# Expert results scattered one expert later, in sets of five transfers that wait once for the first products, with places and gates copied by VectorE

## The chip, the cores and the metric

One core of one Trainium2 chip runs the whole program. The metric is the device time of one execution in microseconds; the number given for a kernel is the median of its runs. A profile is one execution more, with a trace of every instruction.

## The reference, cut to what matters

The program is one pre-norm transformer block on x of shape (4, 1024, 128), 4096 tokens: a windowed attention, then a mixture of experts. Only the second part is touched by the change.

```python
x = x + attention(layernorm(x))
xf = layernorm(x).reshape(4096, 128)
shared = silu(xf @ sg) * (xf @ su) @ sd
# router: 4 of 32 experts per token, gates = softmax of their scores,
# each expert takes at most capacity = 640 (token, choice) pairs
h = silu(einsum('ecd,edh->ech', buf, wg)) * einsum('ecd,edh->ech', buf, wu)   # 256 hidden
out_e = einsum('ech,ehd->ecd', h, wd)
routed[token] += gate * out_e[expert, place]
x = x + shared + routed
```

## The kernel before, in words

**What the stages are.** Up to about 400 us the attention runs (16 pairs of 128-token tiles, software pipelined), together with the router. GpSimd sends every token row, with its pair number and its gate behind it (130 numbers), to its slot in `expert_slots` in DRAM by indirect DMAs (L479). Then come the 32 experts, and last the combination: the four results of each token are loaded from `pair_results` (L425), added to x (L1450, L1456, L1140, L1142) and stored (L798).

**One expert.** An expert has 640 slots, five tiles of 128 rows (`ST` = 5), and hidden width 256, two halves h. `lagged_steps` calls `expert_step(en, e, ed)` on TensorE, VectorE and ScalarE with three experts at once: `en` is one ahead (its slots are turned round and split in two parts), `e` is the present one (products with the gate and the up weights), and `ed` is one behind (product with the down weights, and the results read out). A call is named a stage below. The stages 3 and later run in a hardware loop of two stages per turn; buffers come in pairs, chosen by the expert's parity b.

- TensorE in one stage: five transposes of `xg` (L1101), `gate_up(0)` on the first 320 slots (L1090, 12 matmuls: two halves, gate and up, three partial products each), the down product of `ed` (L1116, 10 products recorded as 20 matmuls), `gate_up(1)` on the other 320 slots (12 more). Each quarter of a `gate_up` adds one to `gu_done`; the last matmul of the down product adds one to `down_done`. The down product waits for `h_mul` (all products of `ed`) and for `y_evac` (the banks of the expert before have been read out).
- ScalarE in one stage: the cast of the weights of `en` (L768), `silu(0)` (two times L761), then the results of `ed` out of the banks, times their gates, into `yout` (five times L780), then `silu(1)` (two times L761). L780 waits for `down_done` and for `y_sent[b]`, which says that the results that stood in this `yout` buffer have landed in DRAM.
- VectorE in one stage: the places of `ed` as whole numbers, `yidx` (L1470), four operations that split `xgT` (L1479, L1482), the products `times_up(0)` (two times L1464, one `h_mul` each), the split of the weights (L1489), `times_up(1)`, and the copy of places and gates from `xg` into `ypair` (L1497), which lets SyncE load the next slots into `xg`.
- GpSimd does nothing but the scatter: for each expert five indirect DMAs (L605) that write the rows of `yout` to `pair_results` at the places in `yidx`. Each one waits for its own tile of results (`y_evac`), so that the first one leaves behind the first L780. The fourth also waits for `h_mul` to reach 4e + 8, which is the last product of expert e + 1.
- SyncE loads the slots (L331), the gate and up weights (L324, L325) and the down weights (L328). L328 waits for `down_done`, so its start shows when SyncE saw that semaphore.

In numbers of experts: while stage e runs, L780 reads out expert e - 1, and GpSimd scatters expert e - 1 in the same stage.

The lines that set the order around the change:

```python
def silu(ch): ... act.wait_ge(S.gu_done, ...); a.activation(hact[...], bank[2 + h], Silu)   # L758 to L762
silu(0)
if ed is not None: ...   # wait down_done, y_sent, ypair_ready, then five times L780
silu(1)
```

Of the kernel before, what the change touches and what calls it, by code (L numbers as in the profile page):

```python
# [14 lines left out]
P = 128  # L15
# [20 lines left out]
NE, NGR, TOPG, TOPK = 32, 8, 4, 4  # L36
# [49 lines left out]
def block_kernel(nc, x, w_qkv, w_out, group_c, expert_c, bias, w_g, w_u, w_d, s_g, s_u, s_d, const, out, where, cap):  # L86
# [53 lines left out]
    with ExitStack() as ctx:  # L140
        def sb(name, shape, dt=F32, stack=None):
            return (stack or ctx).enter_context(nc.sbuf_tensor(name, shape, dt))
# [98 lines left out]
        xg = sb("xg", [P, 2, ST, ROW])  # L241
        ypair = sb("ypair", [P, 2, ST, 2])
        yidx = sb("yidx", [P, 2, ST], U32)

# [20 lines left out]
        pos_read slots slot_ready sh_gu sh_act sh_mul sh_down sh_added  # L265
        xgT_done xgT_hi xgT_lo wgu_hi wgu_lo gu_done h_act h_mul down_done y_evac ypair_ready yidx_ready half_sum comb_step sum_done sum_out stored""".split()
        S = namedtuple("Semaphores", names)(*[sem(n) for n in names])
# [14 lines left out]
        def hold(eng):  # L282

            eng.nop(nofuse=True)
# [156 lines left out]
        def _(pool):  # L441
# [152 lines left out]
            pool.wait_ge(S.zeroed, 16 * NZERO)  # L594
            def scatter(e, c, more):
                pool.wait_ge(S.yidx_ready, e + 1)
                for j in range(ST):
                    if j == 3 and more:


                        pool.wait_ge(S.h_mul, 4 * e + 8)

                    pool.wait_ge(S.y_evac, ST * e + (j + 1))
                    hold(pool)
                    g.indirect_dma_start(  # L605
                        out=pairs_d, out_offset=bass.IndirectOffsetOnAxis(ap=yidx[:, c, j:j + 1], axis=0),
                        in_=yout[:, c, j, :], in_offset=None, bounds_check=N * TOPK - 1,
                        oob_is_err=False).then_inc(y_sent[c], 16)

            with pool.Fori(0, NE // 2 - 1) as i:  # L610
                for c in range(2):
                    scatter(2 * i + c, c, True)
            scatter(NE - 2, 0, True)
            scatter(NE - 1, 1, False)


        @block.scalar
        def _(act):
# [138 lines left out]
            def expert_step(en, e, ed):  # L757
# [11 lines left out]
                if e is not None:  # L769

                    wait(act, S.down_done, e.n - 1)
                    silu(0)
                if ed is not None:
                    act.wait_ge(S.down_done, ed.n + 1)

                    wait(act, y_sent[ed.b], 16 * ST * ed.half)
                    act.wait_ge(S.ypair_ready, ed.n + 1)
                    hold(act)
                    for j in range(ST):
                        a.activation(yout[:, ed.b, j], bank[6 + j // 4][:, j % 4 * D:(j % 4 + 1) * D], ACT.Copy,  # L780
                                     scale=ypair[:, ed.b, j, 1:2]).then_inc(S.y_evac, 1)
                if e is not None:
                    silu(1)

# [362 lines left out]
        def _(dve):  # L1147
# [310 lines left out]
            def expert_step(en, e, ed):  # L1458
# [7 lines left out]
                if ed is not None:  # L1466

                    dve.wait_ge(S.ypair_ready, ed.n + 1)
                    wait(dve, y_sent[ed.b], 16 * ST * ed.half)
                    v.tensor_copy(yidx[:, ed.b], ypair[:, ed.b, :, 0]).then_inc(S.yidx_ready, 1)  # L1470
                if en is not None:
# [19 lines left out]
                if e is not None:  # L1491
                    times_up(1)
                if en is not None:

                    wait(dve, S.yidx_ready, en.n - 1)
                    wait(dve, S.y_evac, ST * (en.n - 1))
                    v.tensor_copy(ypair[:, en.b], xg[:, en.b, :, D:ROW]).then_inc(S.ypair_ready, 1)  # L1497
# [37 lines left out]
```

## Time and profile before

| | us |
|---|---|
| median of 3 runs | 732.65 (728.56 to 733.83) |
| the profiled execution's own time | 729.37 |
| its span in the trace | 726.9 |
| TensorE busy | 574.7 (79%) |
| VectorE busy | 421.1 (58%) |
| ScalarE busy | 323.7 (45%) |
| GpSimd busy | 344.3 (47%) |
| mean granted clock | 0.893 |

A row of the timeline gives the start, the length, the engine, the line and the tiles of one instruction, or of several of the same kind in a row (x2 and so on, with the length from the first start to the last end), and in brackets how long the engine had been idle before it and who ended that. Starts are measured; the ends of matmuls are modelled. SPq is SyncE's own queue. "Remote" or "an unknown queue" is a releaser that the profile could not name. L605 is POOL's part of one transfer; the data moves later.

### The profile page before, as it was taken

The numbers are of one execution on the slowest core, as the hardware profiler recorded it, in microseconds if no ns is written. First come the engines' busy times: TensorE is split into PE (matmuls) and PEld (weight loads), VectorE is DVE, ScalarE is ACT, GpSimd is POOL, SyncE is SP. The second block draws the span as 40 slices with busy tenths as digits, with TensorE's granted clock in tenths as the row PEclk, the third lists the DMA queues.
The fourth block names the chain that finished last, engine by engine and source line by source line (L and its number), as shares of the span: only waits on it lengthen the run. The fifth ranks groups of instructions, "written<-read, shape, count | busy, mean of one in ns | idle before, by whom it ended". The sixth has DMA issues, their size and how long they took to land.

```text
span 726.9 us, 20783 instructions
## 1 busy us (share of the span) xinstructions
PE 574.7 (79%) x7427; PEld 463.1 (64%) x7427; DVE 421.1 (58%) x1284; ACT 323.7 (45%) x830; POOL 344.3 (47%) x393
## 2 busy tenths in 40 slices
PE   2559887888888898777658898788888888888775
PEld 1336665666666666555435787678887888787653
DVE  4757696776787778654445744444444444444155
ACT  4326764665655656445433333444333333333310
POOL 6210034555554445556577055555555555555610
PEclk9669998998888889998989999999999889999897
DMA  9987877865555554300000333332334433332069
GB/s 284 227 233 189 212 209 217 256 184 168 137 157 171 173 159 122 96 20 18 11 9 9 96 115 98 99 87 82 111 99 121 132 118 110 117 88 76 16 249 334
DMA packets 78649, 98.33 MB, mean 135 GB/s; under 512 B 11329, under 2 KB 59231, under 8 KB 78448
## 3 DMA queue, kind: packets, MB, share of 16 engines
q1 hardware_dynamic: 64512, 82.91, 39.7%
q0 software_dynamic: 9216, 12.02, 5.3%
q10 hardware_dynamic: 4848, 2.40, 1.1%
q8 instruction: 49, 0.80, 0.5%
q14 instruction: 24, 0.20, 0.1%
HBM read 50.00 MB, written 54.30 MB: 143 GB/s over the span
## 4 chain that ended last, share of the span: by engine, by line
PE 47%; another core or an unknown queue 13%; issue 12%; ACT 11%; DMA 5%; SPq 5%; DVE 4%; POOL 2%; ACTq 1%; POOLq 0%; DVEq 0%
PE banks L1090 8%; PE banks L1116 6%; PE banks L907 6%; ACT yout L780 4%; DMA rload<-pair_results 3%; PE banks L857 3%; PE banks L978 3%; ACT hact L761 3%; PE banks L849 2%; PE banks L875 2%; SPq L352 2%; PE banks L925 2%; PE banks L888 2%; PE banks L881 2%
## 5 line engine op out<-in xcount | busy, mean ns | idle before, releaser
L605 POOL DMA_INDIRECT pair_results<-yout,yidx x160 | 156.0, 975 | 138.0 <-ACT yout L780 95.2
L479 POOL DMA_INDIRECT expert_slots<-xfe,sidx x128 | 126.0, 984 | 135.1 <-DVE mx L1204 52.3
L1090 PE MATMUL banks<-xgT_parts,wgu_parts 128*128 128x320 f32 x768 | 148.0, 345 | 35.6 <-ACT hact L761 32.9
L1090 PEld LDWEIGHTS banks<-xgT_parts,wgu_parts 128*128 128x128 f32 x768 | 126.1, 208 | 46.9 <-ACT hact L761 36.8
L1464 DVE TENSOR_TENSOR hact<-hact,banks 128x320 f32<-128x320 f32 x128 | 57.0, 481 | 137.2 <-ACT hact L761 126.2
L780 ACT ACTIVATE yout<-banks,ypair 128x128 f32<-128x128 f32 x160 | 44.7, 371 | 135.1 <-remote 79.3
L1204 DVE TENSOR_REDUCE mx<-banks 128x8 f32<-128x1024 f32 x64 | 78.1, 1221 | 37.3 <-PE banks L857 36.4
L648 ACT ACTIVATE pt<-banks 128x512 f32<-128x512 f32 x128 | 69.7, 598 | 51.3 <-PE banks L888 33.4
L1116 PE MATMUL banks<-wdn,hact 128*128 128x128 f32 x640 | 82.3, 287 | 1.9 <-DVE hact L1464 1.9
L1116 PEld LDWEIGHTS banks<-wdn,hact 128*128 128x128 f32 x640 | 82.0, 206 | 2.2 <-issue 2.2
L907 PE MATMUL banks<-pt,vals 128*32 128x64 f32 x2048 | 58.2, 235 | 22.0 <-issue 19.4
L761 ACT ACTIVATE hact<-banks 128x320 f32<-128x320 f32 x128 | 53.3, 452 | 37.6 <-PE banks L1090 26.6
L907 PEld LDWEIGHTS banks<-pt,vals 128*32 128x32 f32 x2048 | 41.2, 117 | 35.1 <-issue 28.0
L525 POOL TENSOR_TENSOR pout<-pin,powers 128x6 f32<-128x6 f32 x16 | 22.3, 1395 | 50.5 <-DVE pin L1285 50.4
L857 PE MATMUL banks<-kS,qS 64*64 64x128 bf16 x1024 | 35.0, 231 | 13.3 <-issue 13.3
L857 PEld LDWEIGHTS banks<-kS,qS 64*64 64x64 bf16 x1024 | 26.9, 114 | 24.8 <-issue 19.7
L653 ACT COPY pvT<-banks 128x512 f32<-128x512 f32 x32 | 18.7, 585 | 53.5 <-PE banks L907 47.3
L849 PE MATMUL banks<-maskq_b,ident_b 64*64 64x512 bf16 x256 | 27.6, 422 | 13.7 <-DVE mx L1204 8.8
L1479 DVE CAST xgT_parts<-banks 128x512 fp32r<-128x512 f32 x64 | 28.3, 483 | 4.7 <-issue 3.3
L1101 PE MATMUL banks<-cst,xg 128*128 128x128 f32 x160 | 25.6, 274 | 6.0 <-issue 3.5
L978 PE MATMUL banks<-cst,pvT 128*128 128x128 f32 x128 | 25.6, 366 | 4.6 <-ACT pvT L653 4.5
L888 PE MATMUL banks<-qS,kS 64*128 64x64 bf16 x1024 | 28.7, 200 | 0.1
(155 smaller groups left out, 957.7 us busy)
## 6 DMA issues: line engine op xcount, KB each, us to landing
expert_slots<-xg SPq DMA_DIRECT2D x8, 1300.0 KB, 9.5
xg<-expert_slots SPq DMA_DIRECT2D x32, 325.0 KB
pair_results<-zero SPq DMA_DIRECT2D x8, 1024.0 KB
rload<-pair_results SPq DMA_DIRECT2D x16, 512.0 KB, 9.5
kS<-rotated_keys SPq DMA_DIRECT2D x32, 240.0 KB
qS<-rotated_queries SPq DMA_DIRECT2D x32, 192.0 KB
wgu<-in_L_ffn_wg_dram SPq DMA_DIRECT2D x32, 128.0 KB
wgu<-in_L_ffn_wu_dram SPq DMA_DIRECT2D x32, 128.0 KB
```

The lines of the kernel that those rows point to most:

```text
L479: g.indirect_dma_start(out=slots_d, out_offset=bass.IndirectOffsetOnAxis(ap=sidx[:, m % NB, j, k:k + 1], axis=0), in_=xfe[:, m % NB, j, k, ...
L605: g.indirect_dma_start(out=pairs_d, out_offset=bass.IndirectOffsetOnAxis(ap=yidx[:, c, j:j + 1], axis=0), in_=yout[:, c, j, :], in_offset= ...
L648: a.activation(pt[:, u], bank[2 + st][:, :], ACT.Exp, scale=QK_SCALE).then_inc(S.exp_done, 1)
L761: a.activation(hact[:, e.b, h, ch * CH:(ch + 1) * CH], bank[2 + h][:, 0:CH], ACT.Silu)\
L780: a.activation(yout[:, ed.b, j], bank[6 + j // 4][:, j % 4 * D:(j % 4 + 1) * D], ACT.Copy, scale=ypair[:, ed.b, j, 1:2]).then_inc(S.y_evac, 1)
L857: last = mm(bank[st][hb * WIN:(hb + 1) * WIN, i * P:(i + 1) * P], qS[rows, p % NX, 4 * c + i, at:at + WIN], kS[rows, p % NX, 4 * c + i, at ...
L907: last = mm(bank[6][32 * (h % 4):32 * (h % 4 + 1), to:to + WIN], vals[:, m % 2, j, hb, h, :], pt[:, 4 * j + NS * c + st, at:at + WIN], sta ...
L978: last = nc.tensor.transpose(bank[6 + j][:, q * P:(q + 1) * P], pvT[:, j, q * P:(q + 1) * P], ident)
L1090: last = mm(bank[2 + 2 * w + h][:, 0:CH], wgu_parts[:, e.b, wp, w, h * P:(h + 1) * P], xgT_parts[:, e.b, xp, ch * CH:(ch + 1) * CH], start ...
L1116: last = mm(bank[6 + j // 4][:, j % 4 * D:(j % 4 + 1) * D], hact[:, ed.b, h, j * P:(j + 1) * P], wdn[:, ed.b, h, :], start=(h == 0), stop= ...
L1204: v.tensor_reduce(mx[:, j, :, 4 * c:4 * c + 4], bank_pairs[0][:, :, :].rearrange("p s (c j) -> p s c j", c=4), AX.X, ALU.max).then_inc(S.p ...
L1464: v.tensor_tensor(hs, hs, bank[4 + h][:, 0:CH], ALU.mult).then_inc(S.h_mul, 1)
```

## The change

It does five things, all in the expert stages.

- ScalarE does `silu(0)` and `silu(1)` first and reads out the results of `ed` after them.
- A second small buffer `ysend` takes the pair (place, gate) from `ypair`. VectorE fills it at the start of a stage (L1469 of the changed kernel), after the read-out of the expert before is over. L780 takes its gates from there (it is L782 now).
- The whole-number places `yidx` are made at the end of a stage, after `times_up(1)` (L1495), with the wait for `y_sent`.
- The copy into `ypair` waits for `ysend` of the expert that stood there, no longer for `y_evac` and `yidx`.
- GpSimd waits once per expert, then issues five transfers without a wait between them. It waits for `h_mul` to reach 4p - 2 with p = e + 3, which is the second product of expert e + 2 (its `times_up(0)`), for `yidx` and for all five tiles of `y_evac`. So expert e is scattered in stage e + 2. For the last two experts p is 32, so that the experts 29, 30 and 31 all wait for the second product of expert 31.

```diff
-            def scatter(e, c, more):
+            def scatter(e, c, half, more, products):
+                pool.wait_ge(S.h_mul, 4 * products - 2)
                 pool.wait_ge(S.yidx_ready, e + 1)
+                pool.wait_ge(S.y_evac, ST * (e + 1))
+                hold(pool)
                 for j in range(ST):
-                    if j == 3 and more:
-                        pool.wait_ge(S.h_mul, 4 * e + 8)
-                    pool.wait_ge(S.y_evac, ST * e + (j + 1))
-                    hold(pool)
                     g.indirect_dma_start(
...
                 if e is not None:
                     wait(act, S.down_done, e.n - 1)
                     silu(0)
+                    silu(1)
                 if ed is not None:
                     act.wait_ge(S.down_done, ed.n + 1)
                     wait(act, y_sent[ed.b], 16 * ST * ed.half)
-                    act.wait_ge(S.ypair_ready, ed.n + 1)
+                    act.wait_ge(S.ysend_ready, ed.n + 1)
...
-                                     scale=ypair[:, ed.b, j, 1:2]).then_inc(S.y_evac, 1)
-                if e is not None:
-                    silu(1)
+                                     scale=ysend[:, ed.b, j, 1:2]).then_inc(S.y_evac, 1)
...
                 if ed is not None:
                     dve.wait_ge(S.ypair_ready, ed.n + 1)
-                    wait(dve, y_sent[ed.b], 16 * ST * ed.half)
-                    v.tensor_copy(yidx[:, ed.b], ypair[:, ed.b, :, 0]).then_inc(S.yidx_ready, 1)
+                    wait(dve, S.y_evac, ST * (ed.n - 1))
+                    v.tensor_copy(ysend[:, ed.b], ypair[:, ed.b]).then_inc(S.ysend_ready, 1)
...
                 if e is not None:
                     times_up(1)
+                if ed is not None:
+                    wait(dve, y_sent[ed.b], 16 * ST * ed.half)
+                    dve.wait_ge(S.ysend_ready, ed.n + 1)
+                    v.tensor_copy(yidx[:, ed.b], ysend[:, ed.b, :, 0]).then_inc(S.yidx_ready, 1)
                 if en is not None:
-                    wait(dve, S.yidx_ready, en.n - 1)
-                    wait(dve, S.y_evac, ST * (en.n - 1))
+                    wait(dve, S.ysend_ready, en.n - 1)
                     v.tensor_copy(ypair[:, en.b], xg[:, en.b, :, D:ROW]).then_inc(S.ypair_ready, 1)
```

GpSimd in the loop over the experts, one expert before (what stands in brackets are the semaphores that the row waits for):

```order
L603 ISA [waits yidx_ready]
L605 DMA pair_results<-yout,yidx 16384x128 [waits y_evac]
L603 REGISTER_ALU
L605 DMA pair_results<-yout,yidx 16384x128 [waits y_evac]
L603 REGISTER_ALU
L605 DMA pair_results<-yout,yidx 16384x128 [waits y_evac]
L601 ISA
L603 REGISTER_ALU [waits h_mul]
L605 DMA pair_results<-yout,yidx 16384x128 [waits y_evac]
L603 REGISTER_ALU
L605 DMA pair_results<-yout,yidx 16384x128 [waits y_evac]
```

Each transfer has its own wait, and the fourth waits for products. The same engine and place in the changed kernel:

```order
L599 REGISTER_ALU [waits h_mul]
L600 REGISTER_ALU [waits yidx_ready]
L603 DMA pair_results<-yout,yidx 16384x128 [waits y_evac]
L603 DMA pair_results<-yout,yidx 16384x128 x4
```

All waits stand ahead of the first transfer now, and the one for products comes first.

ScalarE at the head of the loop, as a piece of the difference (minus is before, plus the changed kernel; L761 is the silu, L780 and L782 the read-out of the results):

```order
-L761 ACTIVATE hact<-banks 128x320 x2
-L780 ACTIVATE yout<-banks,ypair 128x128 x5
-L761 ACTIVATE hact<-banks 128x320 x2
+L761 ACTIVATE hact<-banks 128x320 x4
+L782 ACTIVATE yout<-banks,ysend 128x128 x5
 L768 CAST wgu_parts<-wgu 128x512
```

The read-out moved behind the second pair of silus. VectorE between two stages of the loop:

```order
-L1497 COPY ypair<-xg 128x10
-L1470 CAST yidx<-ypair 128x5
...
+L1495 CAST yidx<-ysend 128x5
+L1498 COPY ypair<-xg 128x10
+L1469 COPY ysend<-ypair 128x10
+L1478 CAST xgT_parts<-banks 128x512
```

One small copy was added, and the making of `yidx` went ahead of the copy into `ypair`.

## Rows read from the trace of the kernel before

**Rows 1.** The page: the chain that ended last, by engine.

```profile
PE 47%; another core or an unknown queue 13%; issue 12%; ACT 11%; DMA 5%; SPq 5%; DVE 4%; POOL 2%; ACTq 1%; POOLq 0%; DVEq 0%
```

**Rows 2.** Who waited for whom, 420 to 688: us in total, times, longest.

```profile
ACT yout L780 <- remote: 79.3, 17, 5.0
ACT yout L780 <- PE banks L1116: 48.7, 13, 4.3
```

**Rows 3.** Timeline of one stage of the loop, and the next read-out.

```profile
488.70 1.40 ACT L780 ACTIVATE yout<-banks,ypair 128x128 f32<-128x128 f32 x5 [4.26 <-PE banks L1116]
489.89 0.97 POOL L605 DMA_INDIRECT pair_results<-yout,yidx  x1 [2.63 <-ACT yout L780]
491.16 0.97 POOL L605 DMA_INDIRECT pair_results<-yout,yidx  x1 [0.30 <-issue]
491.35 0.16 DVE L1497 COPY ypair<-xg 128x10 f32<-128x10 f32 x1
492.51 2.39 PE L1116 MATMUL banks<-wdn,hact 128*128 128x128 f32 x20
493.08 0.87 DVE L1464 TENSOR_TENSOR hact<-hact,banks 128x320 f32<-128x320 f32 x2
494.66 2.00 PE L1090 MATMUL banks<-xgT_parts,wgu_parts 128*128 128x320 f32 x12
494.99 0.97 POOL L605 DMA_INDIRECT pair_results<-yout,yidx  x1 [0.30 <-issue]
497.32 0.38 SPq L328 DMA_DIRECT2D wdn<-in_L_ffn_wd_dram  x1
497.41 1.40 ACT L780 ACTIVATE yout<-banks,ypair 128x128 f32<-128x128 f32 x5 [4.70 <-remote]
```

**Rows 4.** Timeline of the first stages of the loop of experts, no transfer of GpSimd under way.

```profile
416.77 2.39 PE L1116 MATMUL banks<-wdn,hact 128*128 128x128 f32 x20
419.28 1.40 ACT L780 ACTIVATE yout<-banks,ypair 128x128 f32<-128x128 f32 x5 [2.31 <-PE banks L1116]
423.05 2.39 PE L1116 MATMUL banks<-wdn,hact 128*128 128x128 f32 x20
427.92 1.40 ACT L780 ACTIVATE yout<-banks,ypair 128x128 f32<-128x128 f32 x5 [4.13 <-remote]
```

**Rows 5.** Timeline in the attention, around one single transfer.

```profile
204.88 0.78 PE L907 MATMUL banks<-pt,vals 128*32 128x64 f32 x35 [0.42 <-issue]
205.50 0.97 POOL L479 DMA_INDIRECT expert_slots<-xfe,sidx  x1 [0.95 <-ACT xfe L714]
206.93 0.59 ACT L653 COPY pvT<-banks 128x512 f32<-128x512 f32 x1 [1.52 <-PE banks L907]
```

**Rows 6.** Timeline of the stage in which the transfers stopped after three.

```profile
610.79 1.40 ACT L780 ACTIVATE yout<-banks,ypair 128x128 f32<-128x128 f32 x5 [4.98 <-remote]
616.13 0.49 DVE L1464 TENSOR_TENSOR hact<-hact,banks 128x320 f32<-128x320 f32 x1 [0.49 <-PE banks L1090]
617.09 0.98 POOL L605 DMA_INDIRECT pair_results<-yout,yidx  x1 [1.59 <-issue]
618.51 1.40 ACT L780 ACTIVATE yout<-banks,ypair 128x128 f32<-128x128 f32 x5 [2.70 <-PE banks L1116]
622.24 0.97 POOL L605 DMA_INDIRECT pair_results<-yout,yidx  x1 [0.30 <-issue]
624.30 0.49 DVE L1464 TENSOR_TENSOR hact<-hact,banks 128x320 f32<-128x320 f32 x1 [2.41 <-PE banks L1090]
628.72 1.40 ACT L780 ACTIVATE yout<-banks,ypair 128x128 f32<-128x128 f32 x5 [3.14 <-PE banks L1116]
```

**Rows 7.** Windows: busy of PE, PEld, DVE, ACT, POOL, granted clock, DMA share, GB/s.

```profile
420.00:680.00 260.00, 221.17 (x1463) 206.88 (x1462) 121.79 (x325) 100.97 (x297) 146.27 (x150) 0.92 0.35 102
```

**Rows 8.** Timeline of the end of the experts.

```profile
677.62 0.49 DVE L1464 TENSOR_TENSOR hact<-hact,banks 128x320 f32<-128x320 f32 x1 [1.09 <-ACT hact L761]
693.73 0.97 POOL L605 DMA_INDIRECT pair_results<-yout,yidx  x1 [0.30 <-issue]
```

More of the change, by code:

```diff
@@ L242, in block_kernel @@
         ypair = sb("ypair", [P, 2, ST, 2])
+        ysend = sb("ysend", [P, 2, ST, 2])
         yidx = sb("yidx", [P, 2, ST], U32)
@@ L265, in block_kernel @@
         pos_read slots slot_ready sh_gu sh_act sh_mul sh_down sh_added
-        xgT_done xgT_hi xgT_lo wgu_hi wgu_lo gu_done h_act h_mul down_done y_evac ypair_ready yidx_ready half_sum comb_step sum_done sum_out stored""".split()
+        xgT_done xgT_hi xgT_lo wgu_hi wgu_lo gu_done h_act h_mul down_done y_evac ypair_ready ysend_ready yidx_ready half_sum comb_step sum_done sum_out stored""".split()
         S = namedtuple("Semaphores", names)(*[sem(n) for n in names])
@@ L608, in scatter @@
                         oob_is_err=False).then_inc(y_sent[c], 16)
-            with pool.Fori(0, NE // 2 - 1) as i:
+            for e in range(2):
+                scatter(e, e, 0, True, e + 3)
+            with pool.Fori(0, NE // 2 - 2) as i:
                 for c in range(2):
-                    scatter(2 * i + c, c, True)
-            scatter(NE - 2, 0, True)
-            scatter(NE - 1, 1, False)
+                    scatter(2 * i + (c + 2), c, i + 1, True, 2 * i + (c + 5))
+            scatter(NE - 2, 0, NE // 2 - 1, True, NE)
+            scatter(NE - 1, 1, NE // 2 - 1, False, NE)
         @block.scalar
```

## The prediction

> **What bounds the kernel now.** The chain that ended last, on the page, is 47% TensorE and 13% "another core or an unknown queue" [rows 1]. A program on one core has no other core, so the first question is who that is. The list of who waited for whom answers: over the expert stages ScalarE stood 79.3 us ahead of L780 for a "remote" releaser and 48.7 us for L1116 [rows 2]. Together that is 128 us in 30 read-outs, more than half of every stage.
>
> The timeline of one stage shows what it waited for. L780 begins at 488.70 and at 497.41 [rows 3], and over the 23 stages from 427.92 [rows 4] to 628.72 [rows 6] the mean distance is 200.80 / 23 = 8.73 us. Follow the piece at 497.41 back. It needs the down product, whose last matmul is modelled to end at 492.51 + 2.39 = 494.90. TensorE did not stop there: gate_up(1) starts at 494.66. Yet L780 starts only at 497.41, and SyncE, which waits for the same `down_done` and for nothing of `yout`, starts L328 at 497.32 [rows 3]. Two engines see `down_done` at the same moment, 2.4 us after the product. What ends just before? The last of GpSimd's five transfers began at 494.99, 2.33 us before L328. In the stages before any transfer, the same product ends at 416.77 + 2.39 = 419.16 and L780 follows at 419.28, after 0.12 us [rows 4]. So TensorE's `down_done` reaches the others only when a running set of transfers is over. One transfer alone does it too: in the attention L907 ends at 205.66, a transfer starts at 205.50, and the copy that waits for L907 starts at 206.93, 1.43 us after that transfer and 1.27 us after the product [rows 5].
>
> With this the stage closes on itself: read-out to first transfer 489.89 - 488.70 = 1.19, five transfers 494.99 - 489.89 = 5.10, last transfer to next read-out 497.41 - 494.99 = 2.42. The sum is 8.71, the stage. TensorE alone would be faster: with no transfer under way two down products stand 423.05 - 416.77 = 6.28 us apart [rows 4], at the full clock; at the mean granted clock of 0.92 [rows 7] that is 6.8. It idles for the rest.
>
> **The change part by part.** *Read-out behind silu(1).* No cost of its own, the same seven instructions. It takes 1.40 us [rows 3] out from between gate_up(1) and `times_up(1)`; behind the five L780 now stand the weights' cast and `silu(0)` of the next stage. The next down product needs `y_evac`; it comes 6.3 us after the present one at the earliest, and the read-out ends, by the rows' lengths, about 2.4 + 2.0 + 0.5 + 1.4 = 6.3 us after the present one began. Just covered; if not, some tenths.
>
> *Places and gates by VectorE.* One more copy of 0.16 us per expert (as L1497 [rows 3]), 32 x 0.16 = 5 us of an engine that was busy 121.79 of 260 us [rows 7]. It lies ahead of the casts of the next expert, whose result is needed a stage later. I count 0. The move of `yidx` behind `times_up(1)` costs 0: GpSimd needs it a half stage later. Queued behind its wait for `y_sent` are L1498 and through it SyncE's next slots; the set it asks for was sent more than a stage earlier, and 7.4 us after its start it has landed.
>
> At 491.35 a fp32 copy of VectorE (L1497) ran inside a transfer of GpSimd at 491.16, and both kept their lengths, 0.16 and 0.97 [rows 3]. The Trainium skill ("SBUF — State Buffer", the box on "DVE blocks DMA" in "SBUF: two separate sides") says that such a copy locks GpSimd out of the shared port, so that descriptors cannot be written. By that rule each added copy could delay a set by its 0.16 us, 29 x 0.16 = 4.6 us in the sum; the trace shows no such delay, and the sum goes by the trace.
>
> *Transfers one expert later.* This is the term that counts. Before, a set began 1.19 us after the read-out and ran beside the down product and gate_up(1). Now it begins after `times_up(0)`. In rows 3 that ends at 493.08 + 0.87 = 493.95, and from such a product to a waiting transfer it is 617.09 - (616.13 + 0.49) = 0.47 us [rows 6]. So a set starts 493.95 + 0.47 - 492.51 = 1.9 us after the down product began, and lasts 5.10 + 2.33 = 7.4 us until TensorE's messages are through. Within that lie the end of the down product, gate_up(1), the transposes and the next gate_up(0). The loop is now: last part of gate_up(0) seen, `times_up(0)`, five transfers, and again. Bounds for it:
> - Nothing that matters is held: TensorE at the mean clock, 6.8, hardly over GpSimd's own 5 x 1.27 = 6.4.
> - The last part of gate_up(0) is held to the end of the set, as `down_done` is now: 5.10 + 2.33 + 0.49 (the product) + 0.47 = 8.4. If the third part is held as well, a silu of the same 128x320 tile comes in, taken as long as the product: 8.9.
> - gate_up(1) is held as well. That is what the stage of rows 6 shows, the one in which the transfers halted for 1.59 us and then went on at 617.09, 1.2 us after the down product had begun: a product of `times_up(1)` came only at 624.30, 2.06 us after the last transfer at 622.24, and the stage took 628.72 - 618.51 = 10.2.
>
> Which? In rows 3 results that fell in the first part of a set were used at once: gate_up(0) was over when the down product began at 492.51, 2.6 us into the set, and its products ran at 493.08. What was held, the down product at 494.90, fell 5.0 us into it. Of the new stage gate_up(0) falls there, from about 4 us after the set's start on (the rest of the down product 0.5, gate_up(1) 2.0, the transposes, then quarter by quarter). That is the middle case, 8.4. But stages differ: the one up to 618.51 took 618.51 - 610.79 = 7.7 [rows 6], and where a set starts late against TensorE, gate_up(0) slips ahead of the held part. I take two stages of three at 8.4 and one at 7.7, mean 8.2.
>
> *Sum.* From 8.73 to 8.2 in 28 stages: -15. The first set leaves a stage later, so one stage more runs as those of rows 4: -2. At the end experts 29, 30 and 31 all wait for the second product of expert 31, at 677.62 + 0.49 = 678.11 [rows 8]. If the 15 transfers follow closely, the last starts at 678.11 + 0.47 + 14 x 1.27 = 696.4, against 693.73 [rows 8]: +2.7. If each set waits for a held down product, there is one set of 5.1 us and one gap of 2.33 + 1.19 more in it, so up to +7. I take +4, and nothing hides it: the final loads wait for the last transfer. Together -13. The profiled execution took 729.4, 3.3 below the median of 732.65; 729.4 - 13 = 716.4 stands for 719.7 on the scale of the medians. I say 720.
>
> **The rivals.**
> - *TensorE takes over (F).* Held messages fall where nobody waits, and a stage takes 6.8 to 7.4. For it: gate_up(0) was free for 4 us of each set. Against it: the set is longer than TensorE's whole work for a stage, so something always falls in its last part. 28 x (8.73 - 7.1) = 46 less, with the start and the end 44: 689. The Trainium skill ("TensorE: Matmul & The Clock Gate", "The cost: per-tile semaphore tail") gives for a matmul's semaphore a tail of some tens of ns, 25 + 4.7 + 26.3 = 56 for one; by that nothing would be held at all, and this rival would be the forecast. The 2.4 us of rows 3 contradict it here beside transfers; the 0.12 of rows 4 agrees without them.
> - *A wait takes the place of the one removed (N).* Two parts are held, the stage is 8.6 to 8.9, or the late read-out keeps the down product waiting. 28 stages give -3 to +5, start and end +2: 732 to 740, and 728 where the end costs nothing.
> - *gate_up(1) is held (S), slower.* One mechanism: the last quarter of gate_up(1) is not seen before the set is over; then `times_up(1)`, the next down product, VectorE's four operations for the next expert and `times_up(0)` all queue behind it before GpSimd may start. Rows 6 price it at 10.2 for a stage. Such a stage costs 1.5 more than before where the others gain 0.53, so with +2 for start and end it decides from a share s with 28 x (1.5 s - 0.53 (1 - s)) + 2 = 0, s = 0.23. At half of the stages it is 28 x 0.49 + 2 = +16, 748; at all of them 776. For it: only there did a set start so shortly after a down product at full clock, as it will now. Against: a late set shifts itself away from gate_up(1), since the set waits for products and TensorE does not.
> - *The change doesn't do what it says (P).* The 15 transfers at the end and the first stage can't eat more than 7 us, so it isn't a case of its own; it belongs to N.
>
> **How the numbers follow.** Forecast 0.40 (710 to 728: faster by over 1% in 0.32 of it, the rest within), F 0.12, N 0.20 (0.16 within 1%, 0.04 above), S 0.28. One per cent, 7.3 us, is about what a measurement of this kernel can tell from no change. Faster by over 1%: 0.32 + 0.12 = 0.44. Within 1%: 0.08 + 0.16 = 0.24. Slower: 0.04 + 0.28 = 0.32. The range leaves out F's lower half and the part of S with more than half of the stages: 702 to 750. The likeliest case's own range is 710 to 728.
>
> **What would show it.** Right: ScalarE's wait ahead of the read-out (128 us) is gone or small; the first transfers of two sets stand 8.2 to 8.4 apart; VectorE waits ahead of the second product of `times_up(0)` until about 2.3 us after a fifth transfer; the last transfer starts between 696 and 701 less the gain. F: the sets stand 6.8 to 7.4 apart and TensorE has no gaps. S: VectorE's wait ends 2.1 us after the fifth transfer ahead of `times_up(1)`, TensorE waits in gate_up(0) for L1464, and sets stand over 9 us apart. The forecast would be wrong at its root if TensorE's results were seen late with no transfer under way, or at once in the last part of a set.

## The result and the profile after

The changed kernel takes 759.4 us (median of 4 runs, 756.97 to 762.92) beside 733.24 for the kernel before (728.56 to 737.79). The ratio is 1.044, with a 95% interval of 1.0384 to 1.0495: slower, outside the range of the prediction. Ratios here and below are taken over undisturbed executions alone and so can differ a little from the ratio of the medians. The profiled execution has a span of 755.2 us, 28.3 more than before, at a mean clock of 0.876.

The list of who waited for whom (us in total, times, longest), 420 to 715:

```profile
ACT hact L761 <- remote: 111.6, 21, 11.8
POOL pair_results L603 <- DVE hact L1464: 111.4, 18, 24.2
DVE hact L1464 <- ACT hact L761: 88.9, 35, 10.2
```

The same list of the kernel before has for GpSimd, 420 to 688:

```profile
POOL pair_results L605 <- ACT yout L780: 94.9, 30, 19.8
POOL pair_results L605 <- DVE hact L1464: 2.8, 2, 2.5
```

The "remote" wait of [rows 2] has moved from the read-out to the silu, and single waits are longer, 11.8 us against 5.0. GpSimd waited for read-outs before, 94.9 us, and hardly for products (2.8 us). Now it stood 111.4 us for products. The window that answers to [rows 7]:

```profile
420.00:710.00 290.00, 219.71 (x1473) 205.82 (x1471) 128.14 (x357) 103.34 (x306) 146.24 (x150) 0.88 0.30 91
```

TensorE is as busy as before (219.71 against 221.17), in 30 us more. The granted clock is lower (0.88 against 0.92), but the time was lost in idling and not in longer work. The timeline of one of the bad stages, against [rows 3]:

```profile
463.01 1.39 ACT L782 ACTIVATE yout<-banks,ysend 128x128 f32<-128x128 f32 x5
463.49 0.97 POOL L603 DMA_INDIRECT pair_results<-yout,yidx  x1 [3.13 <-DVE hact L1464]
463.69 2.00 PE L1090 MATMUL banks<-xgT_parts,wgu_parts 128*128 128x320 f32 x12
465.53 2.39 PE L1116 MATMUL banks<-wdn,hact 128*128 128x128 f32 x20
467.79 0.49 DVE L1464 TENSOR_TENSOR hact<-hact,banks 128x320 f32<-128x320 f32 x1 [1.22 <-remote]
468.59 1.14 POOL L603 DMA_INDIRECT pair_results<-yout,yidx  x1 [0.30 <-issue]
470.03 0.97 POOL L603 DMA_INDIRECT pair_results<-yout,yidx  x1 [0.30 <-issue]
475.14 0.97 POOL L603 DMA_INDIRECT pair_results<-yout,yidx  x1 [0.30 <-issue]
477.81 0.77 ACT L761 ACTIVATE hact<-banks 128x320 f32<-128x320 f32 x2 [10.34 <-remote]
477.88 0.38 SPq L329 DMA_DIRECT2D wdn<-in_L_ffn_wd_dram  x1
478.30 3.57 PE L1090 MATMUL banks<-xgT_parts,wgu_parts 128*128 128x320 f32 x12 [6.00 <-ACT hact L761]
478.45 1.40 ACT L782 ACTIVATE yout<-banks,ysend 128x128 f32<-128x128 f32 x5
```

Read it from the product at 467.79. It ends at 468.28, and it is the second product of `times_up(0)`, the trigger of the next set. The running set's fifth transfer begins only at 468.59. So the next set follows without a gap (470.03), and there are ten transfers in a row, from 463.49 to 475.14. The down product ends at 465.53 + 2.39 = 467.92; SyncE (L329) sees it at 477.88, 9.96 us later and 2.74 us after the tenth transfer began. The silus of gate_up(1) wait 10.34 us for the same moment, and the read-outs stand 478.45 - 463.01 = 15.44 us apart. Behind its 6.00 us of idling TensorE needs 3.57 us for a gate_up that took 2.00; the granted clock from 478 to 482 is 0.50, the lower of its two levels.

Not everything is held to the end of the run. The gate_up(0) of 463.69 ends at 465.69, 2.2 us into the set, and its last product starts at 467.79: 2.1 us late, but ahead of the fifth transfer. That is what lets the next set join.

From the read-out at 427.34 to the last at 715.04 there are 30 distances. Eight are of this kind, 14.4 to 15.5 us, together 120.7. The other 22 take (287.7 - 120.7) / 22 = 7.59. Before, the 30 from 427.92 to 687.46 took 259.54, 8.65 each. So most stages gained 1.06 us, and eight lost 6.4: 8 x 6.44 - 22 x 1.06 = +28.2. (One of the 22, near the end, took 11.1; there too two sets join, at 695.42 and 701.80. The other 21 took 7.4.) Of the eight, five are ten transfers joined as above; in the other three the second set begins 7.1 to 7.2 us after the first, as here:

```profile
494.01 0.97 POOL L603 DMA_INDIRECT pair_results<-yout,yidx  x1 [4.56 <-DVE hact L1464]
496.42 2.39 PE L1116 MATMUL banks<-wdn,hact 128*128 128x128 f32 x20
499.11 0.97 POOL L603 DMA_INDIRECT pair_results<-yout,yidx  x1 [0.30 <-issue]
501.15 0.97 POOL L603 DMA_INDIRECT pair_results<-yout,yidx  x1 [1.07 <-issue]
505.43 0.39 SPq L329 DMA_DIRECT2D wdn<-in_L_ffn_wd_dram  x1
506.25 0.97 POOL L603 DMA_INDIRECT pair_results<-yout,yidx  x1 [0.30 <-issue]
508.65 0.62 ACT L782 ACTIVATE yout<-banks,ysend 128x128 f32<-128x128 f32 x2
```

The down product ends at 496.42 + 2.39 = 498.81. SyncE sees it at 505.43, 6.6 us later and ahead of the second set's fifth transfer (506.25). So here the message outlasts the first set but not the second. Why it comes out just there, no run shows.

The end, against [rows 8]:

```profile
711.11 0.97 POOL L603 DMA_INDIRECT pair_results<-yout,yidx  x1 [3.23 <-DVE yidx L1495]
722.59 0.97 POOL L603 DMA_INDIRECT pair_results<-yout,yidx  x1 [0.30 <-issue]
```

The last transfer starts at 722.59 instead of 693.73, 28.9 later. Behind it the program takes 32.6 us to its end (755.2 - 722.59), before 33.2.

### The profile page after: what moved, and what is told of

The parts are those of the page before. It is cut to its first block, busy times and chain, and to the rows that moved or that the text cites. A ratio compares the mean times of both kernels' runs of the same rounds, so it can differ in the third digit from the quotient of the medians.

```text
span 755.2 us, 20577 instructions
## 1 busy us (share of the span) xinstructions
PE 577.3 (76%) x7427; PEld 463.4 (61%) x7427; DVE 427.1 (57%) x1316; ACT 324.9 (43%) x830; POOL 345.8 (46%) x393
## 4 chain that ended last, share of the span: by engine, by line
PE 48%; another core or an unknown queue 13%; issue 12%; ACT 6%; DMA 5%; DVE 5%; SPq 5%; POOL 5%; POOLq 0%; ACTq 0%; DVEq 0%
PE banks L1090 13%; PE banks L907 6%; PE banks L1116 6%; DMA rload<-pair_results 3%; SPq L353 2%; POOL expert_slots L480 2%; PE banks L849 2%; PE banks L875 2%; PE banks L978 2%; PE banks L888 2%; PE banks L925 2%; PE banks L857 2%; PE banks L935 2%; PE banks L881 1%
## 5 line engine op out<-in xcount | busy, mean ns | idle before, releaser
L603 POOL DMA_INDIRECT pair_results<-yout,yidx x160 | 156.0, 975 | 166.7 <-DVE hact L1464 111.4
L1090 PEld LDWEIGHTS banks<-xgT_parts,wgu_parts 128*128 128x128 f32 x768 | 124.1, 205 | 66.4 <-ACT hact L761 45.6
L1464 DVE TENSOR_TENSOR hact<-hact,banks 128x320 f32<-128x320 f32 x128 | 59.7, 483 | 152.7 <-ACT hact L761 89.2
L761 ACT ACTIVATE hact<-banks 128x320 f32<-128x320 f32 x128 | 54.7, 447 | 196.2 <-remote 111.6
L907 PE MATMUL banks<-pt,vals 128*32 128x64 f32 x2048 | 62.9, 236 | 24.8 <-issue 22.9
L907 PEld LDWEIGHTS banks<-pt,vals 128*32 128x32 f32 x2048 | 43.3, 116 | 40.8 <-issue 34.7
L782 ACT ACTIVATE yout<-banks,ysend 128x128 f32<-128x128 f32 x160 | 44.7, 381 | 7.2 <-PE banks L1116 7.2
L857 PE MATMUL banks<-kS,qS 64*64 64x128 bf16 x1024 | 32.3, 230 | 9.1 <-issue 9.1
L875 PE MATMUL banks<-eye_b,maskq_b 64*128 64x512 bf16 x128 | 27.9, 433 | 1.0 <-ACT pt L648 1.0
```

The source lines that it names most:

```text
L603: g.indirect_dma_start(out=pairs_d, out_offset=bass.IndirectOffsetOnAxis(ap=yidx[:, c, j:j + 1], axis=0), in_=yout[:, c, j, :], in_offset= ...
L761: a.activation(hact[:, e.b, h, ch * CH:(ch + 1) * CH], bank[2 + h][:, 0:CH], ACT.Silu)\
L857: last = mm(bank[st][hb * WIN:(hb + 1) * WIN, i * P:(i + 1) * P], qS[rows, p % NX, 4 * c + i, at:at + WIN], kS[rows, p % NX, 4 * c + i, at ...
L907: last = mm(bank[6][32 * (h % 4):32 * (h % 4 + 1), to:to + WIN], vals[:, m % 2, j, hb, h, :], pt[:, 4 * j + NS * c + st, at:at + WIN], sta ...
L1090: last = mm(bank[2 + 2 * w + h][:, 0:CH], wgu_parts[:, e.b, wp, w, h * P:(h + 1) * P], xgT_parts[:, e.b, xp, ch * CH:(ch + 1) * CH], start ...
L1464: v.tensor_tensor(hs, hs, bank[4 + h][:, 0:CH], ALU.mult).then_inc(S.h_mul, 1)
```

## The experiments

One thing must be known for all that follows. On the chips that the experiments got, the kernel before takes 641 to 646 us, not 733. That was not foreseen, and e6 shows what the difference is. Each number below is compared with the kernel before on the same chip. I call it holding when a result of TensorE is seen late by the other engines while transfers run. I write of chips, but the first one was not measured a second time, so it may be the chip or something else of that session. Most expectations have a case for a chip that holds; no experiment got one.

### e6: the kernel before, on such a chip

> The kernel before, unedited, for its trace on the chip that this job gets. Held messages belong to the first chip only (my theory by now): if it takes about 646 us, SyncE's L328 and ScalarE's L780 start within 0.2 us of the down product's end also inside a set of transfers, and the stage is 6.4 to 6.8 us. If it takes about 733, they start 2.3 us after the fifth transfer as in [rows 3]. Rival, the difference lies elsewhere (attention, loads, clock): the stage is 8.7 on either chip and the time is gained before or after the experts.

The kernel is unedited. Measured: 635.7 in one run, beside 642.8 (median of 13) for the same kernel. Its timeline, the answer to [rows 3]:

```profile
489.13 2.39 PE L1116 MATMUL banks<-wdn,hact 128*128 128x128 f32 x20
490.60 0.97 POOL L605 DMA_INDIRECT pair_results<-yout,yidx  x1 [0.30 <-issue]
491.69 0.38 SPq L328 DMA_DIRECT2D wdn<-in_L_ffn_wd_dram  x1
491.71 1.40 ACT L780 ACTIVATE yout<-banks,ypair 128x128 f32<-128x128 f32 x5 [2.39 <-PE banks L1116]
491.88 1.39 POOL L605 DMA_INDIRECT pair_results<-yout,yidx  x1 [0.30 <-issue]
498.05 1.40 ACT L780 ACTIVATE yout<-banks,ypair 128x128 f32<-128x128 f32 x5 [2.32 <-issue]
```

The product ends at 491.52, and SyncE and ScalarE follow 0.17 and 0.19 us later, 1.1 us after a transfer began. In [rows 3] it was 2.4 us, at the end of the set. So here transfers hold nothing, and the stage is 6.59 us (26 distances from 420.39 to 591.73). The 93 us between the last transfers of the two profiled executions (693.73 and 600.49) split into 62.6 in the expert stages and 30.6 ahead of the first transfer of results (420.48 and 389.88). There the attention runs, and its transfers hold messages too [rows 5], but the granted clock also differs, 0.87 against 0.91 over the first 388 us; how the 30.6 divide isn't shown. Why one chip holds messages and the others don't, no run tells.

### e5: the changed kernel, on such a chip

> The changed kernel as it is, beside the kernel before, on the chip that this job gets. In the first four experiments the kernel before took 646 us instead of 733, and in their traces nothing of TensorE's was held. If holding is what made the change slower, then where the kernel before takes about 646 nothing is held, and the changed kernel is at most 2% slower or a little faster: 630 to 660. If the kernel before takes about 733 again, the changed kernel takes 757 to 763 again, and down_done is held as before. Rival, VectorE's copies or the late read-out made it slower: the ratio of 1.044 comes back on any chip, 675 beside 646.

Measured: 644.1 (10 runs) beside 644.5, ratio 0.991 (0.984 to 0.997). So on a chip without holding the change costs nothing. The windows 440 to 590 of the kernel before (first, from e6), of this one, and of e13 (last):

```profile
440.00:590.00 150.00, 143.21 (x1089) 139.57 (x1087) 91.24 (x240) 77.92 (x225) 115.46 (x112) 1.00 0.43 130
```

```profile
440.00:590.00 150.00, 147.35 (x1122) 143.61 (x1120) 102.16 (x270) 79.05 (x231) 114.63 (x117) 1.00 0.44 134
```

```profile
440.00:590.00 150.00, 146.81 (x1136) 145.60 (x1135) 96.41 (x271) 77.90 (x236) 70.46 (x74) 1.00 0.41 122
```

117 transfers in 150 us are 1.28 us each: GpSimd sends without a pause, 6.4 us per stage, and TensorE is busy 147 of the 150.

### e1 and e13: no transfers, and three of five

```diff
# e1: the scatter of the results and the waits for y_sent are left out
-            for e in range(2):
-                scatter(e, e, 0, True, e + 3)
...
# e13: SENT is 3; the waits for y_sent count with it too
-                for j in range(ST):
+                for j in range(SENT):
```

> The changed kernel without GpSimd's transfers of results; everything else, VectorE's copies and the late read-out too, stays. It leaves out the writing of the expert results, so the routed part of the output is missing. Held messages (my theory: what TensorE tells the others is held while a set of transfers is under way, and two sets that join hold it for 14 us): with no transfer nothing is held; stages fall from 9.7 us to TensorE's own 6.3 to 6.8, so 30 x 3 = 90 us less than the changed kernel, and some 20 to 30 less at the end, where three sets were sent in a row: 640 to 680. Late read-out as the cause: the stage stays above 8.7 us in spite of the missing transfers, over 720. VectorE's added copies as the cause: likewise over 720, since they are all still there.

> The changed kernel with three of the five transfers of each set; the results of the tiles 3 and 4 of every expert are not written. Where nothing is held: GpSimd no longer sets the stage (3 x 1.28 = 3.8), TensorE's 6.3 does: 625 to 640, near the 627 without any transfer. Where messages are held: a set holds them for 3 x 1.43 = 4.3 us, inside TensorE's 6.3, and a down product waits little: 670 to 700 instead of 759. Rival, the number of transfers does not matter, only that there is a set: within 1% of the changed kernel.

Measured: 627.4 beside 646.4 (0.968, 0.958 to 0.977), and 628.6 beside 643.0 (0.977, 0.971 to 0.984). The numbers fall below my ranges for e1, which counted with holding. What follows is for chips without holding. All transfers together cost 19 us there, and three per stage are nearly as good as none: the read-outs stand 6.3 us apart in both. GpSimd's 6.4 us per stage is the bound by a little, TensorE's 6.3 the next.

### e11 and e12: a pause behind each transfer

```diff
                        oob_is_err=False).then_inc(y_sent[c], 16)
+                    g.memset(idle[:, j], 0.0).then_inc(S.paused, 1)
+                pool.wait_ge(S.paused, ST * (e + 1))
```

> The changed kernel with a small memset (128x64) of GpSimd behind each transfer, so that two transfers stand further apart than the 1.43 us for which one transfer held TensorE in [rows 5]. Where messages are held (before at about 733): they come out between two transfers, nothing adds up to 7 or 14 us, and the stage is five times the new distance, about 1.5, so 7.5 us: 690 to 715 instead of 759. Where nothing is held (before at about 643): GpSimd's transfers set the stage there (5 x 1.28 = 6.4), and the memset adds 5 x 0.2 per stage: 665 to 680. Rival, GpSimd's transfers do not set the stage there: no change, 638 to 648.

> The kernel before with the same memset behind each transfer. Where messages are held: down_done comes out inside the set, and the stage is 7.5 instead of 8.7: 690 to 710. Where nothing is held: slower than before for the same reason as the changed kernel, 660 to 680.

Measured: 675.9 and 675.1 beside 643.0 (1.048 and 1.047). The times came as expected, but not in the way I had written. The timeline of e11:

```profile
489.44 0.97 POOL L604 DMA_INDIRECT pair_results<-yout,yidx  x1 [0.16 <-issue]
490.41 0.17 POOL L608 MEMSET idle<- 128x64 f32 x1
491.66 0.97 POOL L604 DMA_INDIRECT pair_results<-yout,yidx  x1 [1.07 <-issue]
492.95 0.97 POOL L604 DMA_INDIRECT pair_results<-yout,yidx  x1 [0.16 <-issue]
```

Inside a set the distance is 1.29, not 1.5: the memset fits into the 0.30 us that GpSimd needs anyway. Only between two sets is it 2.22 instead of 1.28. That one us lengthened the stage from 6.4 to 7.6: GpSimd sets it. Whether wider gaps let messages through where they are held was not measured.

### e4, e9, e3: the parts, without holding

```diff
# e4: four more copies of VectorE beside the added one
+                    for k in range(4):
+                        v.tensor_copy(yspare[:, ed.b, k], ypair[:, ed.b]).then_inc(S.spared, 1)
# e9: the kernel before, only silu(1) ahead of the read-out
                     silu(0)
+                    silu(1)
...
-                if e is not None:
-                    silu(1)
# e3: the changed kernel, silu(1) behind the read-out again
                     silu(0)
-                    silu(1)
...
+                if e is not None:
+                    silu(1)
```

> The changed kernel with four further VectorE copies like the added one (128x10, fp32) at the same place in every stage, into a buffer nobody reads. If the added copy cost what the rule of the Trainium skill on the shared port says, or cost through VectorE's place in the chain, four more cost at least 4 x 0.16 x 32 = 20 us: 780. Held messages: VectorE waits for held messages and has room; 0 to 5 us more, 759 to 764.

> The kernel before with one part of the change alone: silu(1) goes ahead of the read-out, the transfers stay where they were. If the late read-out costs by itself, this is over 1% slower than before on any chip; in my step it was 0, so within 1%. With held messages (a chip where before takes 733) it lets silu(1) and times_up(1) run while down_done is held: same or up to 10 us faster. Without holding, the set leaves about 1.4 us later in the stage and nothing waits for it: within 1%.

> The changed kernel with ScalarE's order of before: the read-out stands between silu(0) and silu(1) again. Late read-out as the cause of the loss: the time goes back to that of before, about 733. Held messages: the read-out waits for a held message either way, and now silu(1) queues behind it, so nothing is won and some may be lost: 755 to 780.

Measured: e4 646.6 beside 646.4. Its four runs spread from 638 to 654, so the time alone would not show 10 us; but its read-outs stand 6.44 us apart (440 to 600 of the span), those of the changed kernel in e5 6.43. So VectorE's copies, five of them in each stage, cost nothing that can be seen. e9 649.0 beside 642.8, 1.005 (0.999 to 1.011). e3 668.2 beside 646.4, 1.035 (1.026 to 1.044). The late read-out alone costs about 1% at most; the later transfers without it cost 3.5%. The timeline of e3 shows on what:

```profile
485.98 0.97 POOL L603 DMA_INDIRECT pair_results<-yout,yidx  x1 [0.30 <-issue]
488.71 1.40 ACT L781 ACTIVATE yout<-banks,ysend 128x128 f32<-128x128 f32 x5 [3.28 <-DMA pair_results<-yout,yidx]
```

The set leaves a stage later into the same two `yout` buffers, so the read-out waits until the set that stood in its buffer has landed, 2.7 us after its last transfer. With silu(1) ahead of it that time is used. So the later transfers need the late read-out, while the late read-out can stand alone.

### e2 and e10: the trigger, without holding

```diff
# e2: a set only when the set before has landed
                 pool.wait_ge(S.y_evac, ST * (e + 1))
+                wait(pool, y_sent[1 - c], 16 * ST * (half + c))
# e10: no wait for products
-                pool.wait_ge(S.h_mul, 4 * products - 2)
```

> The changed kernel, with one more wait of GpSimd: a set starts only when the set before it has landed, so two sets can no longer join into ten transfers. Held messages: the down product's message is let through between any two sets, 7.4 us after a set's start; the stages with two joined sets (14 us of holding) are gone. A set then starts at the earliest 5.1 + 2.3 us after the one before, and is still bound to products: 8.2 to 9.2 per stage, 720 to 750, clearly under the changed kernel's 759. Rival, a single set's hold is what costs: no change or slower, 755 to 775, since GpSimd only gets a wait more. Late read-out or VectorE's copies as the cause: no change, 755 to 765.

> The changed kernel, but GpSimd does not wait for products any more: an expert's set leaves as soon as its read-out is over, in sets of five without a wait inside. Where nothing is held, GpSimd sends without a pause in both kernels already (1.28 us per transfer, 6.4 us per stage), so the stages stay at 6.4 and only the end gains, as the last experts no longer queue up: 0 to 12 us less than the changed kernel, 630 to 645. Where TensorE's messages are held, a set starts 1.9 us after the read-out's start and holds the next down_done: 1.9 + 5.1 + 2.4 = 9.4 per stage at most, 735 to 755, with no joined sets. Rival, the late trigger was of use by itself: over 2% slower than the changed kernel's 644 where nothing is held.

Measured: e2 700.8 beside 646.4 (1.084, 1.076 to 1.092); e10 643.1 beside 641.5 (1.004, 1.000 to 1.008). e2 was made for a chip that holds messages and tells nothing of joined sets there; here it stops GpSimd for 2.0 us a stage (36.3 us in 18 waits), and the stage is 6.4 + 2.0 = 8.4. e10 removes the trigger, and the read-outs stand 6.44 us apart, as in e5. The gain of up to 12 us over the changed kernel that I had expected did not show: its ratio to the kernel before was 0.991 in e5, on another chip, and is 1.004 here.

### e7, e8: the holding imitated by a wait

```diff
                     wait(act, y_sent[ed.b], 16 * ST * ed.half)
+                    wait(act, y_sent[1 - ed.b], 16 * ST * (ed.half + ed.b))
```

The read-out also waits until the set of the expert before has landed. It stands for a `down_done` held to the end of that set.

> The kernel before, with one more wait that imitates the holding: ScalarE's read-out of an expert also waits until the whole set of the expert before has landed. On a chip that holds nothing the stage should become 1.19 + 5.10 + 2.4 = 8.7 as in [rows 3], 30 x (8.7 - 6.5) = 66 us more: 700 to 735 instead of 646. Rival, what the first chip lost was not this wait: under 670.

> The changed kernel with the same added wait: the read-out of an expert also waits until the set of the expert before, which now starts later, has landed. A set then starts after times_up(0), holds the read-out for 7.4 us, and 1.40 of read-out and the cast stand ahead of the next silu(0): 9.5 to 11 us per stage, 740 to 790, slower than the kernel before with the same wait. Rival, holding hits both alike: within 1% of the kernel before with the wait.

Measured: 710.2 for the kernel before and 824.7 for the changed one, beside 642.8. With the same added wait the change costs 16%. The timeline of e7:

```profile
484.08 1.40 ACT L781 ACTIVATE yout<-banks,ypair 128x128 f32<-128x128 f32 x5 [4.75 <-DMA pair_results<-yout,yidx]
485.26 0.97 POOL L605 DMA_INDIRECT pair_results<-yout,yidx  x1 [2.64 <-ACT yout L781]
490.37 0.97 POOL L605 DMA_INDIRECT pair_results<-yout,yidx  x1 [0.30 <-issue]
492.71 1.40 ACT L781 ACTIVATE yout<-banks,ypair 128x128 f32<-128x128 f32 x5 [3.79 <-DMA pair_results<-yout,yidx]
```

1.18 + 5.11 + 2.34 = 8.63: term by term the stage of [rows 3]; the mean of the 23 stages from 423.56 on is 8.75 against 8.73. So one wait of this kind is enough to give the stage of before. e8:

```profile
497.77 1.40 ACT L783 ACTIVATE yout<-banks,ysend 128x128 f32<-128x128 f32 x5 [4.83 <-DMA pair_results<-yout,yidx]
499.55 0.80 ACT L761 ACTIVATE hact<-banks 128x320 f32<-128x320 f32 x2
500.14 0.89 DVE L1465 TENSOR_TENSOR hact<-hact,banks 128x320 f32<-128x320 f32 x2 [4.76 <-ACT hact L761]
502.01 0.97 POOL L603 DMA_INDIRECT pair_results<-yout,yidx  x1 [6.77 <-DVE hact L1465]
510.70 0.62 ACT L783 ACTIVATE yout<-banks,ysend 128x128 f32<-128x128 f32 x2 [4.53 <-DMA pair_results<-yout,yidx]
```

Here the loop is longer: between the read-out and the next set stand the rest of the read-out, the cast, silu(0) and `times_up(0)`, 4.24 us instead of 1.18, and from the set to the read-out 8.69. The sum is 12.93. I had expected 9.5 to 11 and 740 to 790 us in all. The imitation is harsher than what happened on the first chip (9.6), for it holds every read-out, where there 22 of 30 stages slipped through at 7.6; and it can't join sets. It also waits for the landing, which in this stage comes 3.6 us after the fifth transfer (507.11), against 2.34 in e7. Some of the 16% is that, and not the longer way to the next set.

### e14, e15, e16: which part makes holding dear

> Imitated holding as in e8 (a read-out also waits until the set of the expert before has landed), on the changed kernel without GpSimd's wait for products. In e8 a stage was 12.8 us: 8.7 from a set's start to the read-out, then 1.4 of read-out, 0.4 to silu(0), 0.6 to times_up(0), 0.9 of it and 1.0 to the next set. If this trigger behind times_up(0) is what makes holding dear, the set now leaves 1.4 + 0.5 us after the read-out's start and the stage is 8.7 + 1.9 = 10.6 at most, 9.4 at least: 740 to 770 instead of 825. Rival, the read-out's late place is what is dear: no change, 815 to 835.

> Imitated holding as in e7, on the kernel before with silu(1) ahead of the read-out, the one part of the change. The loop read-out, five transfers, landing, read-out does not contain silu(1): 705 to 715 as in e7 (710). Rival, the late read-out is what is dear where the read-out is held: over 730.

> Imitated holding as in e8, on the changed kernel with the read-out between the silus again: only the later transfers and VectorE's copies remain. If the later transfers with their trigger are what is dear, it stays near e8 or goes above, as silu(1) too stands behind the read-out now: 820 to 850. If the late read-out was: 710 to 760.

The edits are those of e10, e9 and e3, each with the wait of e7. Measured, in us, each beside 642.8 to 644.0 without the added wait (the stage is the mean distance of read-outs, between 440 and 600 us of the span):

| with the imitated holding | time | stage |
|---|---|---|
| kernel before (e7) | 710.2 | 8.8 |
| before, late read-out (e15) | 713.2 | 8.8 |
| changed, early read-out (e16) | 876.8 | 14.2 |
| changed (e8) | 824.7 | 12.7 |
| changed, no wait for products (e14) | 765.2 | 10.4 |

The late read-out costs nothing that counts. The later transfers cost, and half of the 114.5 us between e7 and e8, 59.5, is the wait for `times_up(0)`; what the other half is was not taken apart. e14 and e15 came as expected; e16 was dearer than the 820 to 850 that I had said. The timeline of e14:

```profile
494.19 1.40 ACT L782 ACTIVATE yout<-banks,ysend 128x128 f32<-128x128 f32 x5 [4.99 <-DMA pair_results<-yout,yidx]
496.41 0.97 POOL L602 DMA_INDIRECT pair_results<-yout,yidx  x1 [4.42 <-ACT yout L782]
```

The set leaves here 2.22 us after the read-out's start instead of 4.24.

## Why the prediction was wrong, step by step

- *What bounds the kernel.* Right, and stronger than the rows allowed to say: the "remote" wait is a `down_done` held by a running set. Where nothing holds it the stage is 6.6 (e6), and one added wait gives 8.75 again (e7). What I could not see is that other chips don't hold. The estimate of 56 ns for one increment, from the Trainium skill's "TensorE: Matmul & The Clock Gate" ("The cost: per-tile semaphore tail"), is nearer to e6, where SyncE starts 0.17 us behind the modelled end, than to the 2.4 us of [rows 3].
- *Read-out behind silu(1), 0.* Right by itself (e9, e15). That it also covers the landing of the later set (e3) was missed: I wrote that the set asked for had been sent more than a stage earlier.
- *Places and gates by VectorE, 0.* Right: four more copies change nothing (e4). The 4.6 us that I estimated by the Trainium skill's rule on the shared port ("SBUF — State Buffer", the box on "DVE blocks DMA" in "SBUF: two separate sides") would be 18 for these four, 0.6 per stage; the stage is 6.44 in e4 and 6.43 in e5, on chips where GpSimd's own pace sets it.
- *Transfers one expert later, -15.* This is the step that failed, at the middle case, "The last part of gate_up(0) is held to the end of the set", and the mean of 8.2 built on it. I treated each set by itself; the measured mean is 9.6. 22 of 30 stages were better than 8.2, at 7.59. But in those TensorE runs ahead: the down product of 488.66 begins 5.3 us into its set (483.38), the next one, 496.42, only 2.4 us into its set (494.01). The next gate_up(0) then falls into the early part of a set, where messages still pass, its products fire the next trigger before the fifth transfer or soon after it, and two sets join or nearly do. No bound of mine had a hold of 14 us: the dearest stage that I priced took 10.2, and eight took 15.1. The rows had a sign of it. I read the transfers of [rows 6], 617.09 to 622.24, as one late set, but they are the last two of one set and the first three of the next, as two more lines of the kernel before show:

```profile
618.38 0.97 POOL L605 DMA_INDIRECT pair_results<-yout,yidx  x1 [0.30 <-issue]
619.69 0.97 POOL L605 DMA_INDIRECT pair_results<-yout,yidx  x1 [0.34 <-issue]
```

  So the stage of 10.2 was itself one in which two sets join. A smaller error stands beside it: from the product to the first transfer I took 0.47 us. In the changed kernel, where the waits stand ahead of that transfer, it is 0.98 (in e8 from 500.14 + 0.89 = 501.03 to 502.01). That makes the middle case 8.9 instead of 8.4, and the forecast some 9 us longer (28 x 2/3 x 0.5).
- *Start and end, +2.* The start gained 0.6 (427.34 against 427.92, two stages free), and the end was 1.3 later behind the last read-out (7.55 against 6.27).
- *The rivals.* S was the right sign and the right message: the silus of gate_up(1) waited 10.34 us. Its argument against, "a late set shifts itself away from gate_up(1), since the set waits for products and TensorE does not", was the error: the set waits for products, and so it comes early as soon as TensorE is early. S's price was too small and its count too large: 8 of 30 stages at 15.1, where it reckoned with 28 (776) or 14 (748) at 10.2. The break-even share for stages at 15.1 against others at 7.6 is (8.65 - 7.59) / (15.09 - 7.59) = 0.14; it was 0.27. F, that TensorE's results are not held where it matters, came true for both kernels on the chips without holding, which is why they are equal there.

What is shown: on the first chip, by the timelines, that sets join, how long messages are held then, and that the eight stages in which two sets follow each other so closely lose more than the others gain; on the chips without holding, that the change costs nothing; and by imitation, that the trigger behind `times_up(0)` makes a held read-out dearer. Argued only: that without the joining the changed kernel would be faster than before on the first chip; e2, made for it, did not run where messages are held. No version beat both kernels: without holding TensorE and GpSimd leave about 3% (e1), and with it none could be tried.

## What to carry to other kernels

Price a wait by the loop that it closes, and ask what happens to that loop when the other engines get faster: a trigger that comes from the engine which is being held can fire into the running burst and double it. When a stall has no cause in the program, measure the same kernel on a second chip before building on the stall. Of two moves that look separate (read-out later, transfers later) one can be the other's cover, so try each with and without the other.

## What the runs showed of the hardware

- The same kernel takes 733 us on one chip and 641 to 646 on four others. Between the profiled executions all of the difference (93 us) lies ahead of the last transfer. In [rows 3] other engines see TensorE's semaphore 2.3 us after the fifth transfer of the set began, 2.4 us behind the down product; in the run of ten above 2.7 us after the tenth, 9.96 us behind the product. In e6 it is seen after 0.2 us.
- On the first chip some came out sooner: of a gate_up(0) that ended 2.2 us into a set (465.69) the last part was used at 467.79, before the fifth transfer, and where a second set began 7.1 us after the first, the down product of 498.81 was seen at 505.43, inside the second.
- On the first chip TensorE itself stopped in such a run, at transposes, with no releaser that the profile could name:

```profile
469.52 0.27 PE L1101 MATMUL banks<-cst,xg 128*128 128x128 f32 x1
470.58 0.49 PE L1101 MATMUL banks<-cst,xg 128*128 128x128 f32 x3 [0.79 <-issue]
472.03 0.27 PE L1101 MATMUL banks<-cst,xg 128*128 128x128 f32 x1 [0.96 <-issue]
```

The distance from the second to the third, 1.45 us, is about that of one transfer in [rows 5] (1.43).
